# Softmax shift and weights as 48 small ScalarE operations in the transformer block of a vision kernel

## The reference

```
scores = jnp.einsum('bhtd,bhsd->bhts', q, k) / jnp.sqrt(jnp.float32(HD))
scores = jnp.where(causal[None, None], scores, jnp.float32(-1e+30))
att = jax.nn.softmax(scores, axis=-1)
y = jnp.einsum('bhts,bhsd->bhtd', att, v).transpose(0, 2, 1, 3).reshape(Bx, Tx, Cx)
```

## Time and profile before

| | us |
|---|---|
| median of three executions | 7286.18 (7277.96 to 7286.59) |
| the profiled execution, its own time | 7289.36 |
| its span in the trace | 7287.6 |
| PE / DVE / ACT / POOL busy in the span | 6652.6 / 4615.7 / 4417.5 / 3746.7 |
| mean granted TensorE clock | 0.953 of full speed |

### The profile page before, as it was taken

The page is one execution under the profiler, slowest core; times in us unless marked ns, Lnnn a source line. Parts: engine busy times, 40 slices in busy tenths (PEclk is TensorE's granted clock), DMA queues, the critical chain, the costliest instruction groups (busy, mean ns, idle before and its releaser), DMA issues. The chain is left out here.

```text
span 7287.6 us, 138653 instructions
## 1 busy us (share of the span) xinstructions
PE 6652.6 (91%) x43858; PEld 4057.5 (56%) x43858; DVE 4615.7 (63%) x7185; ACT 4417.5 (61%) x8385; POOL 3746.7 (51%) x1364
## 2 busy tenths in 40 slices
PE   8999899999899999899999899999999578888888
PEld 3444566666666666666666544444444255555555
DVE  8999577777477776577776333333333477777774
ACT  5666467667467666576675577777777444444443
POOL 8999277787278786377875244444444100000000
PEclk9999999999899999999999999999999778888888
DMA  2333455554555554555554311111111333333330
GB/s 98 111 114 112 173 164 166 167 166 159 179 166 167 167 169 157 182 166 167 166 166 166 105 54 48 48 48 53 49 48 48 105 80 75 75 75 75 74 75 3
DMA packets 595494, 835.11 MB, mean 115 GB/s; under 512 B 450408, under 2 KB 491496, under 8 KB 529768
## 3 DMA queue, kind: packets, MB, share of 16 engines
q1 hardware_dynamic: 595432, 834.33, 36.8%
HBM read 477.60 MB, written 356.58 MB: 114 GB/s over the span
## 5 line engine op out<-in xcount | busy, mean ns | idle before, releaser
L958 POOL TENSOR_TENSOR sb_rstd<-sb_var,sb_minus_half 128x16 f32<-128x16 f32 x1280 | 3690.1, 2899 | 2008.9 <-DVE sb_var L909 1010.9
L700 DVE TENSOR_TENSOR sb_unit<-H,sb_rstd 128x512 f32<-128x512 f32 x768 | 528.8, 688 | 684.4 <-POOL sb_rstd L958 546.2
L517 PE MATMUL H<-sb_conv_block,sb_act_in 128*128 128x128 f32 x6144 | 826.4, 283 | 8.8 <-DVE sb_unit L700 6.8
L517 PEld LDWEIGHTS H<-sb_conv_block,sb_act_in 128*128 128x128 f32 x6144 | 732.6, 192 | 124.6 <-issue 115.4
L622 ACT ACTIVATE sb_act_px<-sb_unit 128x512 f32<-128x512 f32 x768 | 483.9, 630 | 493.0 <-DVE sb_unit L706 492.9
L2328 POOL TENSOR_TENSOR blk_pos<-blk_pos,blk_mag 128x260 f32<-128x260 f32 x32 | 23.0, 738 | 1311.7 <-ACT blk_mag L1983 1311.7
L645 ACT ACTIVATE sb_act_out<-TC 128x512 f32<-128x512 f32 x768 | 447.7, 583 | 181.9 <-PE TC L532 181.9
L921 DVE COPY sb_act_out<-TC 128x512 f32<-128x512 f32 x256 | 176.9, 691 | 595.4 <-PE TC L767 595.4
L784 PE MATMUL M<-sb_dense,sb_fc_w 128*64 128x512 f32 x2048 | 521.5, 608 | 30.5 <-ACT sb_dense L867 25.5
L703 DVE TENSOR_TENSOR sb_unit<-sb_unit,sb_gain_row 128x512 f32<-128x512 f32 x768 | 531.4, 692 | 26.2
L706 DVE TENSOR_TENSOR sb_unit<-sb_unit,sb_shift_row 128x512 f32<-128x512 f32 x768 | 531.3, 692 | 26.1
(11 more groups left out here) (276 smaller groups left out, 12765.2 us busy)
## 6 DMA issues: line engine op xcount, KB each, us to landing
act_scratch<-sb_act_out SPq DMA_DIRECT2D x256, 1024.0 KB, 3.9
sb_act_in<-act_scratch SPq DMA_DIRECT2D x256, 1024.0 KB, 5.3
spectrum_in<-sb_f_sb SPq DMA_DIRECT2D x512, 78.0 KB, 1.8
sb_x_in<-spectrum_in SPq DMA_DIRECT2D x48, 832.0 KB, 4.4
spectrum_out<-sb_y_sb SPq DMA_DIRECT2D x48, 832.0 KB, 4.6
sb_z_in<-spectrum_out SPq DMA_DIRECT2D x512, 78.0 KB, 5.1
blk_rows_b<-scan_rows SPq DMA_DIRECT2D x128, 260.0 KB, 6.4
blk_rows_bb<-scan_rows SPq DMA_DIRECT2D x128, 260.0 KB, 7.4
```

Of the source, the lines that this page charges most:

```text
L517: e.matmul(H[j][:, 128 * u:128 * u + 128], act_in[p][:, 128 * b:128 * b + 128], conv_block[:, :], start=(u == 0), stop=False, skip_group_c ...
L700: e.tensor_tensor(rows, H[k][:, :].rearrange("p (y c) -> p y c", c=C), rstd[k][:, :].unsqueeze(2).to_broadcast([128, 16, C]), ALU.mult).th ...
L958: e.tensor_tensor(rstd[j][:, :], var[j][:, :], minus_half[:, :], ALU.pow).then_inc(rstd_ready, 1)
```

## The change

The subtraction of the maximum for the first half, and both multiplications by the reciprocal, go from DVE to ACT. DVE makes a negated maximum `mneg` of 65 x 16 instead of the first subtraction. ACT then adds it block by block as a bias: 16 `Identity` operations on 65 x 65, four in each of slots 7 to 10, behind that slot's silu. The weights become 32 `Copy` operations with the reciprocal as scale: four in each of slots 12 to 19, one sequence a slot, behind that slot's silu. PE waits in slot 13 + m for the four weights of sequence m instead of waiting twice for a half. The exponential of the first half waits for the 16 `lowered` operations; the second half's subtraction stays on DVE.

```diff
+        mneg = sb("mneg", [T, Q * NH])
...
+        SPAN = 4
...
                     if m < GI:
-                        if m % Q == 0:
-                            wait(e, "weighted", g, m // Q + 1)
+                        wait(e, "weighted", g, NH * (m + 1))
...
                         e.activation(silu[n % 2][:, :], B[0][0:2 * HP, 0:TOK], ACT.Silu).then_inc(sig["silu"], 1)
+                    if attn and SHIFT_AT[0] < n <= SHIFT_AT[0] + SPAN:
+                        wait(e, "depth", ga)
+                        for j in range(NH * Q * (n - SHIFT_AT[0] - 1) // SPAN, NH * Q * (n - SHIFT_AT[0]) // SPAN):
+                            e.activation(sc[:, T * j:T * j + T], sc[:, T * j:T * j + T], ACT.Identity,
+                                         bias=mneg[:, j:j + 1]).then_inc(sig["lowered"], 1)
+                    if attn and TURN_AT - 1 <= n < TURN_AT + GI - 1:
+                        m = n - TURN_AT + 1
+                        if m == 0:
+                            wait(e, "recip", ga)
+                        for j in range(NH * m, NH * m + NH):
+                            e.activation(sc[:, T * j:T * j + T], sc[:, T * j:T * j + T], ACT.Copy,
+                                         scale=rc[:, j:j + 1]).then_inc(sig["weighted"], 1)
                     if attn and n == EXP_AFTER:
...
                         for half in range(2):
-                            wait(e, "shifted", ga, half + 1)
+                            if half:
+                                wait(e, "shifted", ga)
+                            else:
+                                wait(e, "lowered", ga)
...
-                    e.tensor_tensor(rows_h, rows_h, peak_h.unsqueeze(2).to_broadcast([T, Q * NH, T]), ALU.subtract)\
-                        .then_inc(sig["shifted"], 1)
+                    if h == 0:
+                        e.tensor_scalar(mneg[:, :], peak_h, -1.0, None, ALU.mult).then_inc(sig["depth"], 1)
+                    else:
+                        e.tensor_tensor(rows_h, rows_h, peak_h.unsqueeze(2).to_broadcast([T, Q * NH, T]), ALU.subtract)\
+                            .then_inc(sig["shifted"], 1)
...
-                if n in WEIGHT_AT:
-                    h = WEIGHT_AT.index(n)
-                    rows_h, _, _, rc_h = half_of(h)
-                    wait(e, "recip", g)
-                    e.tensor_tensor(rows_h, rows_h, rc_h.unsqueeze(2).to_broadcast([T, Q * NH, T]), ALU.mult)\
-                        .then_inc(sig["weighted"], 1)
```

More of the change, by code:

```diff
@@ L1561, in build_block @@
             a_mean=1, a_cen=1, a_square=1, a_variance=1, a_guess=4, a_newton=6, r=1,
-            un=1, qk=2, v=1, v_copied=1, rope=6, q_image=2, kx=NH, scores=GI, masked=GI, peak=2, shifted=2, expd=2,
-            total=2, recip=1, weighted=2, p_turned=GI, p_copied=GI, yv=Q, y_copied=Q, wo=1, x2=1, residual=1,
+            un=1, qk=2, v=1, v_copied=1, rope=6, q_image=2, kx=NH, scores=GI, masked=GI, peak=2, depth=1, lowered=NH * Q, shifted=1, expd=2,
+            total=2, recip=1, weighted=NH * GI, p_turned=GI, p_copied=GI, yv=Q, y_copied=Q, wo=1, x2=1, residual=1,
             x_square=1, x_variance=1, x_guess=2, x_newton=3, ue=1, router=1, gate=21,
```

## The result

The changed kernel takes 7412.57 us in the median of four executions (7401.98 to 7423.09), against 7286.39. The ratio is 1.0168, with a 95% interval of 1.0155 to 1.018: 126 us slower. A second comparison gave 7403.55 and a ratio of 1.0156 (1.0138 to 1.0175). The profiled execution took 7401.98 us with a span of 7400.2, 112.6 more than the kernel before. The forecast was 7382, with a range of 7342 to 7432.

The account below looks back on a forecast made before the run. No engine is full, so order decides: PE waits for DVE to slot 14 and sets the pace from slot 15. 6.45 in each of windows 1 to 14 (90.3) + 7 - 2 = 95 us: 7382, range 7342 to 7432.

Parts of the forecast that it names:

- The price of the operations: On ACT, 0.345 us for one 65 x 65 operation, 1.07 for four; on DVE, 0.16 for the negation.
- Slots 6 to 9: DVE gains 0.7 us, slot 9's W3 wait shrinks from 1.04 to about 0.35; ACT's operations there cost nothing.
- Slot 10: Four operations between silu 10 and the table load add 1.05 us, less 0.7 from DVE: +0.35 a window.
- The turns: In slots 16 to 20, turns 4, 5 and 7 come 1.3 us later each, +3.9 a window; 3 and 6 covered.
- From W1 of slot 12 to W1 of slot 15: Waits for the weights eat what DVE's relief gives there: +1.2 us a window, between 0 and 2.4.
- The clock: New waits in each window's second half bring one more low-clock stretch: +1.0 us a window, between 0 and 3.
- Window 0: Turn 0 no longer waits for DVE's multiplication: 2 us less, between 3.4 less and 2 more.
- 95: The whole forecast loss in us over all windows, taking the profiled execution from 7289.36 to 7384.7.
- The collapse of the clock: Rival, chance 0.15: low clock holds through slots 13 to 20, 10 us a window, 145 in all, 7431 and up.
- DVE's relief: Rival, chance 0.05: less DVE work up to slot 14 outweighs ACT's operations, 3 to 22 us faster, 7264 to 7283.

Follow-up runs that it names:

- the doubled run: The changed kernel with four more small ScalarE operations, on other data into a spare tile, ahead of each four weights: 7573.7 us, ratio 1.0392.

## Why the prediction was right

- **The price of the operations** held: 0.337 for one against 0.345, 1.05 to 1.06 for four against 1.07, 0.17 for the negation.
- **Slots 6 to 9** held: the wait of slot 9 went from 1.04 to 0.38 in every window, against 0.35 forecast.
- **Slot 10** held in its parts: from silu 10 to silu 11 it is 6604.15 to 6610.15 us, 6.00 against 5.03 before, 0.97 more. In the mean over windows the way to silu 11 was -0.2 instead of +0.35: 0.5 too dear.
- **The turns** held: waits at 1, 2, 4, 5 and 7, none at 3 and 6. They are 0.56 to 1.06 long, where I had 1.27; part of the difference is that the weights start 0.29 behind silu's start and not 0.39. Compared at like clock, a window of 35.25 with 7.0 us low against one of 30.11 with 6.6 before, the stretch costs 5.1 more. From W1 of slot 12 to W1 of slot 15 it is 11.28 against 9.77, 1.5 where I had 1.2, and behind that 3.6 where I had 3.9. The sum fits better than its basis: I took the window with the 1.17 us wait of slot 14 for all, and only four of windows 1 to 13 have it.
- **The clock** was the mis-sized term, and its mechanism was half right. I had the new waits bring the clock down once more a window; the rows show that the low stretch behind silu 11, which was there before, lasts up to 20 us, and a further fall comes in three windows of thirteen only. I priced it at 1.0. The mean window is 38.1 where the one at like clock is 35.25, so 2.9; before, it was 0.5 (30.6 against 30.11). Net 2.4 instead of 1.0. That is 1.4 a window, less the 0.5 that slot 10 was too dear: +0.9 times 14, 13 us.
- **Window 0** got 2.1 slower (71.4 to 73.55 from its start to the next), where I had it 2 faster: 4 us more. Turn 0 does come 1.0 earlier (5840.51 against 5841.53), but without expert work in between, turns 1, 2, 4, 5 and 7 each wait 1.43 for their weights, and turn 7 starts 1.7 later than before.
- 95 + 13 + 4 = 112 agrees with the 112.6 of the profiled execution. The median of the runs lies 11 above that execution, and in the second comparison 9 below the first median. Such a spread, 21 us in four executions, is what a clock that falls in some windows and not in others would give, but I have traces of two executions only (with five and four windows of 40.7), so this is argued and not shown.
- **The rivals.** The collapse of the clock is what the doubled run shows, not the changed kernel, though five of its thirteen windows come near it (20.3 us low). DVE's relief is real, 37 us, and was hidden under the waits. The Trainium skill (TensorE: Matmul & The Clock Gate, What's actually happening) has the clock fall after an idle window. The fall at silu 11 does follow a long wait, of 3.54 us. The falls in mid-flow do not: the one shown came behind a wait of 0.99 us with work around it. By that rule the waits of the turns would cost no clock, yet filling them took the low part from 12.9 to 8.7. The measurement decides: waits with work between them do cost clock.

## What to carry to other kernels

A small operation that moves to an idle engine is not free if it stands between two others of a chain that goes back and forth. Count the time from the producer's start to the consumer's next step, not the engine's load. With the weights issued a slot ahead of their consumer and the shift kept out of slot 10, the same 48 operations go from 126 us slower to 35 us faster. And where TensorE is the bound, price repeated short waits together with the clock that they may keep down: here the clock added about half of the waits' own cost, and in the doubled run more than all of it.

## What the runs showed of the hardware that I had not expected

The kernel sped up when TensorE was given useless products to do in its waits (7403.55 to 7372.61). With five waits of 0.56 to 1.06 us, the part at the low level went from 6.7 us of 30.6 to 13.9 of 38.1; with waits of 1.5 to 2.0 us it was 31 of 50. TensorE once busy again did not get its clock back at once: in one window it was busy 18.9 of 20.48 us, with two waits of 0.56 us among them, and all of that ran at the low level. Within one execution, windows of the same instructions took 35.25 to 40.68 us, and the rows show no other difference than the clock: 5.4 us for 13.3 us more at the low level, 0.41 for each.
